# A fused vision block on one core: third image's turn, projection and skip products inside the scan, alternating PSUM tiles ahead of it

## The reference

```
x = x + L0(_gn(x))   # two depthwise 3x3 convs (g, g1), Sobel, 5 iterations of
                     #   h = D*(c0*h0 - 2*E*h + cm_x*roll(h,1,2) + cp_x*roll(h,-1,2)
                     #          + cm_y*roll(h,1,3) + cp_y*roll(h,-1,3)) + D*2*DT*fsrc, then bn + relu
x = x + L1(_gn(x))   # 3x3 conv, 64 -> 64 channels
x = x + L2(_gn(x))   # Mamba block: layernorm, in_proj (x and z), causal conv of 4 taps, silu,
                     #   dt/B/C projections, softplus, selective scan over 1024 tokens with 16 states,
                     #   y*silu(z), out_proj, + skip*x_norm, layernorm, proj
x = x + L3(_gn(x))   # 2-D DCT of 32 x 32
```

## Time and profile before

| | us |
|---|---|
| median of 3 runs (987.44 to 994.75) | 987.76 |
| the profiled execution | 989.86 |
| its span, first to last instruction | 987.7 |
| PE / DVE busy | 807.9 / 798.5 |
| ACT / POOL busy | 564.3 / 519.6 |
| mean granted TensorE clock, share of full speed | 0.948 |

### The profile page before, as it was taken

One profiled execution on the slowest core, in us unless ns is written; L12 is line 12 of the kernel. 1 busy time (PEld: TensorE's weight loads), 2 busy tenths in 40 slices (PEclk: granted clock), 3 DMA queues, 4 the chain that ended last, 5 costly groups with the idle time before them and its releaser, 6 DMA issues. The chain is left out here.

```text
span 987.7 us, 10385 instructions
## 1 busy us (share of the span) xinstructions
PE 807.9 (82%) x3787; PEld 509.9 (52%) x3787; DVE 798.5 (81%) x652; ACT 564.3 (57%) x983; POOL 519.6 (53%) x240
## 2 busy tenths in 40 slices
PE   3999998976576778799999999797756677869995
PEld 2444443443365667656545444344335577865654
DVE  6899885377998998998899888447699999899832
ACT  3755231146479897786667332114456979878712
POOL 2015993110498786876111699311048869677730
PEclk8999999999799999899999999898869989989988
DMA  3000000001535454443000000000123445444400
GB/s 104 1 0 0 0 0 1 0 1 48 133 134 180 153 181 163 140 159 130 20 0 11 12 0 0 1 0 1 48 89 127 175 148 184 160 148 154 146 21 22
DMA packets 32878, 73.95 MB, mean 75 GB/s; under 512 B 15544, under 2 KB 15680, under 8 KB 32832
## 3 DMA queue, kind: packets, MB, share of 16 engines
q1 hardware_dynamic: 31424, 72.04, 21.9%
q0 software_dynamic: 320, 1.05, 0.4%
q10 hardware_dynamic: 1088, 0.26, 0.1%
HBM read 70.71 MB, written 2.62 MB: 74 GB/s over the span
## 5 line engine op out<-in xcount | busy, mean ns | idle before, releaser
L338 POOL TENSOR_TENSOR arena<-arena 128x1024 f32<-128x1024 f32 x128 | 304.8, 2392 | 99.1 <-DVE arena L1603 72.8
L1603 DVE TENSOR_TENSOR_SCAN arena<-arena,ps 128x1024 f32<-128x1024 f32 x128 | 290.1, 2282 | 20.6 <-ACT arena L857 9.6
L857 ACT ACTIVATE arena<-arena 128x128 f32<-128x128 f32 (+3 forms) x424 | 157.1, 446 | 91.3 <-DVE arena L1530 75.3
L857 ACT ACTIVATE arena<-arena,Amat 128x1024 f32<-128x1024 f32 x128 | 145.3, 1145 | 62.0 <-DVE arena L1603 61.1
L544 PE MATMUL ps<-mat,arena 128*128 128x128 f32 x528 | 74.8, 288 | 51.6 <-DVE arena L1603 49.9
L857 ACT ACTIVATE arena<-ps 128x1024 f32<-128x1024 f32 (+2 forms) x62 | 56.1, 917 | 93.7 <-PE ps L414 29.0
L717 PE MATMUL ps<-arena,mat 128*128 128x512 f32 x240 | 106.3, 592 | 0.0
L586 PE MATMUL ps<-mat,arena 128*128 128x128 f32 x768 | 104.7, 281 | 1.1 <-POOL arena L338 0.8
L544 PEld LDWEIGHTS ps<-mat,arena 128*128 128x128 f32 x528 | 60.9, 144 | 67.3 <-DVE arena L1603 53.3
L586 PEld LDWEIGHTS ps<-mat,arena 128*128 128x128 f32 x768 | 90.9, 146 | 3.3 <-POOL arena L338 2.3
L1598 DVE TENSOR_TENSOR ps<-arena,ps 128x1024 f32<-128x1024 f32 x66 | 80.0, 1213 | 3.5 <-PE ps L544 3.5
(11 more groups left out here) (186 smaller groups left out, 1374.3 us busy)
## 6 DMA issues: line engine op xcount, KB each, us to landing
arena<-c_rows SPq DMA_DIRECT2D x128, 512.0 KB, 3.8
out<-arena SPq DMA_DIRECT2D x28, 64.0 KB, 2.2
xres<-x POOLq DMA_DIRECT2D x4, 256.0 KB, 5.3
xres<-x SPq DMA_DIRECT2D x4, 256.0 KB, 4.1
convw<-conv_w SPq DMA_DIRECT2D x1, 576.0 KB
c_rows<-ROWS SPq DMA_DIRECT2D x4, 128.0 KB, 1.9
mat<-mats SPq DMA_DIRECT2D x1, 448.0 KB, 3.7
inw<-in_w SPq DMA_DIRECT2D x1, 256.0 KB
```

The costliest lines, as they stand in the source:

```text
L338: tt(HC[s % 2], HS[s % 2], CB[s % 4], ALU.mult).then_inc(S("hc"), 1)
L857: return nc.scalar.activation(out_, in_, func, bias=bias, scale=scale, accum_out=accum_out)
L1603: nc.vector.tensor_tensor_scan(HS[q], DA[q], PS[q][:, :], 0.0, ALU.mult, ALU.add).then_inc(S("scan"), 1)
```

## The change

It edits these things at once:
- X_STEPS: for s from 9 to 25 the odd steps instead of s % 5 in (0, 2, 4), so 9 instead of 11 there.
- Ahead of the scan: new tiles `x_ps(k, b)` and `z_ps(k, b)` alternate with the image; `in_proj` is split into `x_in_proj` (second image waits for the first image's `silu_z`, semaphore sz) and `z_in_proj` (second image waits for rx); `bc_proj`, `keep_rows` and the first rows' turn use PS[2k] and PS[0]; the orders on TensorE, ScalarE and VectorE are rewritten; `relu_x(h, 1, 1)` moves behind `scan_step(h, 1)`; the spins go from 8 + 14 to 8 + 10 products.
- `bnout` of stage 0 writes PS[2k + 1] instead of the SBUF tile X, and `add_stage0` reads it there.
- Image 3 is turned too: `sum_of` takes the transposing form for all, `turn_y(h, 3)` and `keep_y(h, 3)` come before `out_proj(h, 3)`.
- Image 2 is turned at s = 49 (waits for X3) and kept by ScalarE at s = 51; the DCT of pair 0 moves up by one to three steps; `skip(1)` goes to s = 61 and `out_proj(h, 2)` to s = 62; TensorE waits for `y_kept(h, 2)` at s = 50.
- The centring's sums come at s = 38, `small_mean` at s = 40.
- Between the halves: `frames` before the first taps on ScalarE; `gate(3)` between Sobel's two parts; `write_all(PS[3])` and its wait (a_open 7) for `first_tap(1, 1, 0)`; `x_neighbours(h, 0)` directly behind `y_neighbours(h, 0)`; the second half's two rolls of pair 0 by 8 DMAs on SP's queue in place of two products and two copies; `from_D(h, 1)` stays behind `seed(h, 0)`.

```
-        X_STEPS = [s for s in range(9, SCANS - 1) if (s % 5 in (0, 2, 4) if s < 3 * D_STATE else s % 2 == 1)]
+        X_STEPS = [s for s in range(9, SCANS - 1) if (s % 5 in (0, 2, 4) if 26 <= s < 3 * D_STATE else s % 2 == 1)]
+        def x_ps(k, b):
+            return PS[2 * k + b]
+        def z_ps(k, b):
+            return PS[2 * k + 1 - b]
-        TURNED = [0, 1, 2]
+        TURNED = [0, 1, 2, 3]
...
+            def roll_by_dma(dst, src, up):
+                for g in (0, C):
+                    here, there = (g + 1, g) if up else (g, g + 1)
+                    sp.dma_start(dst[here:here + C - 1, :], src[there:there + C - 1, :]).then_inc(S("rolled"), 16)
+                    edge, other = (g, g + C - 1) if up else (g + C - 1, g)
+                    sp.dma_start(dst[edge:edge + 1, :], src[other:other + 1, :]).then_inc(S("rolled"), 16)
+            def roll_first_pair(h):
+                a = A[0]
+                sp.wait_ge(S("a_Py"), 4 * h + 2)
+                sp.wait_ge(S("a_Pm"), 2 * h + 1)
+                roll_by_dma(a["Kx"], a["Pmy"], up=False)
+                roll_by_dma(a["Ky"], a["R"], up=True)
@@ SyncE, end of a half @@
                 store_out(h, 0)
+                if h + 1 < HALVES:
+                    roll_first_pair(h + 1)
                 store_out(h, 1)
@@ TensorE, new calls @@
+            def x_in_proj(h, k, b):
+                pe.wait_ge(S("xnc"), 2 * h + k + 1)
+                if b == 1:
+                    pe.wait_ge(S(f"sz{k}"), 2 * h + b)
+                for n in range(2):
+                    last = mm(half(x_ps(k, b), n), inw[:, 2 * P * b:2 * P * b + P], half(D[k]["XNC"], n), start=True, stop=True)
+                last.then_inc(S(f"xi{k}"), 1)
+            def z_in_proj(h, k, b):
+                pe.wait_ge(S("xnc"), 2 * h + k + 1)
+                if b == 1:
+                    pe.wait_ge(S(f"rx{k}"), 2 * h + b)
...
@@ TensorE, ahead of the scan, the new order @@
+                group_mean(D[1], h, 2, 1)
+                spin(PS[1], 10)
+                n2_pixels(h, 1)
                 xn_channels(h, 0)
+                x_in_proj(h, 0, 0)
+                z_in_proj(h, 0, 0)
+                x_in_proj(h, 0, 1)
+                xn_channels(h, 1)
                 dt_proj(h, 0, 0)
+                x_in_proj(h, 1, 0)
+                z_in_proj(h, 1, 0)
                 dt_proj(h, 0, 1)
+                x_in_proj(h, 1, 1)
+                dt_proj(h, 1, 0)
+                z_in_proj(h, 0, 1)
+                z_in_proj(h, 1, 1)
                 bc_proj(h, 0)
                 turn_first_rows(h)
+                dt_proj(h, 1, 1)
                 pe.wait_ge(S("b_kept"), h + 1)
                 plain(pe)
                 b_rows(h, 0)
+                pe.wait_ge(S("rx0"), 2 * h + 2)
                 b_rows(h, 1)
                 bc_proj(h, 1)
                 b_rows(h, 2)
+                pe.wait_ge(S("rx1"), 2 * h + 2)
@@ TensorE, in the scan and behind it @@
+                    if s == 49:
+                        pe.wait_ge(S("X3"), 2 * h + 1)
                         turn_y(h, 2)
...
+                    if s == 50:
+                        y_kept(h, 2)
                         group_mean(D[0], h, 3, 0)
+                    if s == 52:
                         x3_pixels(h, 0)
+                    if s == 54:
                         first_dct(h, 0)
+                    if s == 56:
+                        a2_pixels(h, 0)
+                    if s == 57:
                         keep_x3(h, 0)
+                    if s == 58:
                         second_dct(h, 0)
+                    if s == 61:
+                        pe.wait_ge(S("ot"), 2 * h + 1)
+                        skip(1)
+                    if s == 62:
+                        out_proj(h, 2)
...
                 sum_of(h, SCANS - 1)
-                out_proj(h, 2)
+                turn_y(h, 3)
                 if h + 1 < HALVES:
                     depthwise(h + 1, 0, 0, 0)
                 out_proj(h, 3)
+                if h + 1 < HALVES:
+                    write_all(PS[3])
@@ VectorE, ahead of the scan, the new order @@
                 add_conv(h, 1)
+                x2_norm(h, 1)
                 normalize(0, h, 0)
                 center(1, h, 0)
                 variance(1, h, 0)
+                causal(h, 0, 0)
                 normalize(1, h, 0)
                 causal(h, 0, 1)
                 causal(h, 1, 0)
+                relu_x(h, 0, 0)
+                causal(h, 1, 1)
                 relu_x(h, 1, 0)
                 one_plus(h, 0)
                 one_plus(h, 1)
                 first_relu_part(h)
                 one_plus(h, 2)
+                relu_x(h, 0, 1)
                 delta(h, 0)
                 first_delta_u(h)
                 dve.wait_ge(S("first_du"), 2 * h + 2)
                 scan_step(h, 0)
                 delta(h, 1)
                 scan_step(h, 1)
+                relu_x(h, 1, 1)
                 delta(h, 2)
@@ ScalarE, ahead of the scan, the new order @@
                 norm2(h, 0)
                 square(h, 0, 0)
+                norm2(h, 1)
                 layer_scale(h, 0)
+                square(h, 1, 0)
                 silu_z(h, 0, 0)
                 silu_x(h, 0, 0)
                 layer_scale(h, 1)
                 silu_x(h, 0, 1)
                 silu_z(h, 1, 0)
+                abs_x(h, 0, 0)
                 abs_x(h, 0, 1)
                 silu_x(h, 1, 0)
                 abs_x(h, 1, 0)
+                silu_z(h, 0, 1)
                 for j in range(3):
                     exp_of(h, j)
                 silu_z(h, 1, 1)
                 silu_x(h, 1, 1)
+                keep_rows(h, 0)
+                ln_of(h, 0)
+                ln_of(h, 1)
+                keep_first_b(h)
+                ln_of(h, 2)
                 decay(h, 0)
                 keep_rows(h, 1)
                 decay(h, 1)
+                abs_x(h, 1, 1)
                 decay(h, 2)
@@ ScalarE, before the iteration loop, and stage 0's result @@
+                    if h > 0 and k == 0:
+                        act.wait_ge(S("rolled"), 128)
+                        act.sem_inc(S("a_Q5"), 1)
+                        act.sem_inc(S("a_Q6"), 1)
+                        act.wait_ge(S("a1_gg1"), 2 * h + 2)
+                        field(0)
+                        act.wait_ge(S("a_Pe"), 2 * h + 1)
+                        seed(h, 0)
+                        from_D(h, 1)
+                        continue
...
-                    av(img(a["X"]), wrapped(a["hw"])[:, :, 1:33], ACT.Relu, par[:, 4:5], par[:, 5:6]).then_inc(S("a_bnout"), 1)
+                    av(img(PS[2 * k + 1]), wrapped(a["hw"])[:, :, 1:33], ACT.Relu, par[:, 4:5], par[:, 5:6]).then_inc(S("a_bnout"), 1)
@@ ScalarE, end of a half @@
+                if h + 1 < HALVES:
                     act.wait_ge(S("X3"), 2 * h + 1)
                     zero_framed(h + 1, 0)
+                    frames(h + 1, 0)
                     first_tap(h + 1, 0, 0)
                     first_tap(h + 1, 0, 1)
+                    keep_y(h, 3)
                     squares(h + 1, 0)
                     zero_framed(h + 1, 1)
```

## The result

The changed kernel took **966.71 us** (median of 4 runs, 965.02 to 967.41) against 988.8 for the kernel before, measured beside it; the ratio is 0.976, 95% interval 0.973 to 0.980. Predicted were 966.0 and 957 to 979. The profiled execution took 966.85 us with a span of 964.9, so 22.8 us of span are to be explained. The total is right; most of its terms are not, and that their errors cancel to 1.1 us is luck.

A forecast was written before the change was run, and what follows sets the result against it. TensorE and VectorE were taken to share most of the span, GpSimd to bound the loop, with waits ahead of the scan. Terms 11.8 + 2.8 - 0.6 + 3.0 + 2.6 + 1.1 + 1.05 = 21.75 us gave 966.0, range 957 to 979.

The forecast's parts named there:

- Ahead of the scan: Conv's end to first scan: second image's product no longer waits for the first's `relu_x`; 5.9 us a half, 11.8 gained.
- The walk: New orders ahead of the scan timed instruction by instruction from the conv's end: first scan at 51.1 us, before 58.3.
- Stage 0's addition: VectorE's addition with one operand in PSUM takes 1.2 us; 1.9 gained in first half, 0.9 in second, 2.8 together.
- X steps: Scan: two fewer X steps a half add 4.9 us of multiplications, but waits for GpSimd go; net -0.6 us.
- Centring: In the scan, sums at s = 38 let scan 39 cover `small_mean`; 1.5 us a half, 3.0 gained.
- End of the scan: Image 3's sum takes 1.0 instead of 1.72 us, giving TensorE room for moved work; 2.6 us for both halves.
- Between the halves: Last scan of first half to second loop: loop starts 2.4 us earlier, 1.3 already counted, so 1.1 gained.
- The charge of 2 us for the clock: Between the halves: 2 us of TensorE work charged for running at 1.2 GHz after 5 us of idle.
- Tail: Last scan's end to the centring of pair 1: 8.75 us instead of 9.8, so 1.05 gained.
- Rival A: New order ahead of the scan waits elsewhere, half of 11.8 lost: 972, or 976 with X steps at worst; 22%.
- B: Between the halves, DMA rolls land late and hold up `field(0)` and the loop: 972, at the high bound 987; 9%.
- C: TensorE falls to 1.2 GHz ahead of the scan: +17 us a half, 1000, slower; 4%.

## Why the prediction was right, and where it wasn't

**Ahead of the scan, 11.8 forecast, 15.6 measured.** The mechanism is right: with its own tile the second image's product no longer waits. The step that fails is the choice of the value: the second half's 4.5 us stood in the bounds, not in the sum. The same instructions took 4.5 us longer there than in the first half before the change, at a clock of 0.86, where two of the second images' products took 3.75 and 3.28 us instead of 1.95. In the new order one group a half is slow (3.4 to 3.5 us), and VectorE loses 0.9 us to it or less. That the order does it is shown by the experiment on the order alone; why TensorE keeps the higher clock in it is not, for idle times of 2.49 and 2.86 us remain.

The walk itself was 2.0 to 2.4 us too short (51.1; 53.5 and 53.1 measured). In both halves 1.0 is missing at the start: VectorE waits 2.18 us for the turns of both pairs, which stand together ahead of the first x (12.4 instead of 11.4). In the second half a slow `dt(0,0)` holds the third `causal` back by 0.93. In the first half it was the place that the prediction named, `keep_rows(0)`: ScalarE waited 1.39 us there for slow products, and the first scan came 0.5 later than in the halves without it, not 2.

**Stage 0's addition, 2.8 forecast, 0.9 or less measured** by putting it back (0.5 and 0.4, inside what executions vary). The duration was right. The step "behind it stands `new_h(1)`, which waits for GpSimd's last addition: 1.9 remains" named the wrong releaser: TensorE's last product of the loop came later than GpSimd.

**X steps, -0.6 forecast, -2.3 in the two traces, -3.0 by putting them back (3.5 in the edited steps).** The traces' -2.3 holds a gain of 1.1 that is not theirs: in the second half the order ahead of the scan alone brings steps 2 to 26 from 77.21 to 76.07. The multiplications were counted right; the step that fails is the waits said to go with them. Those for GpSimd were to fall by 3.7 and fell by 0.9 in the first half and 0.6 in the second (2.2 to 1.6), and the wait of 1.39 for ScalarE at step 11, behind its two copies of the next half's input (290.53 to 292.76), is new.

**Centring, 3.0 forecast, 4.0 measured by putting it back.** 1.5 a half, as worked out, and some 0.4 more by step 50 that I had not counted.

**End of the scan, 2.6 forecast, 4.95 measured.** Half by the cheaper sums, half by the schedule. The sum took only the last wait of 1.23; four smaller ones in steps 57 to 61, 1.8 us a half together, gave place to one of 0.97.

**Between the halves, 1.1 forecast, 0.95 measured.** The loop starts 86.30 us behind the last scan instead of 87.25 (85.6 to 87.6 in the traces with this order, so the agreement proves little). The charge of 2 us for the clock, line 1526 at 1.22 us and the centring that stays all hold. GpSimd's two products, now beside operations of VectorE that read PSUM, took 2.20 us each instead of 3.05 and 3.19, and none of those operations was longer than 1.23, so the 2 us that the port rule might have cost did not arise. The rolls took 9.3 us, not 7.6 (5.5 us lie between SP's first and last issue), and filled the whole cover of 9.4. The sign "`field(0)` not released by a DMA" failed: ScalarE waited 1.81 us for the landing. The estimate of 18.4 us for the eight, one behind the other, came from the Trainium skill, "DMA: Bandwidth & Descriptors" ("Anatomy of one DMA"), whose figures are for transfers issued by GpSimd; these were issued by SyncE, and the traces show 9.3 and 10.5 us.

**Tail, 1.05 forecast, -1.26 measured.** The value that I set as a bound (-2, lower clock) was the case. The step that fails is the price of the three TensorE pieces: 1.0, 1.1 and 1.9 us in the sum, 1.94, 1.97 and 3.67 measured. The 5 us of idle that I priced between the halves stand here too, in pieces of 2.08, 1.32 and 1.11 us that I did not add up to anything.

So the sum is 1.1 us short of 22.8 because +3.8 (ahead), +1.2 (centring) and +2.4 (end of the scan) met -1.9 (first half's addition), -1.7 (X steps), -0.3 (second addition, between the halves) and -2.3 (tail). Rival A is out (9.3 us of waiting is left, not over 10), B came within 0.1 us of deciding, C is out: the clock ahead of the scan was 0.94 in both halves, and its slow products cost 0.5 to 0.9 us a half there. The range's low end is off as well: 966.0 less 4.5 and 3.2 is 958.3, not 957. And two halves of 1.25 at the end of the scan are 2.5, not 2.6.

## What to carry to other kernels

TensorE's clock is part of the schedule: moving real work out of a gap can cost as much as it saves. Unread products paid where every TensorE piece stands on the chain (the tail: 2.4 to 3.4 us for 13 of them, and 2.0 for ten more in the last stage); ahead of the scan they were worth 0.5 us a half at most, and between the halves nothing that the time shows. Ask of a filler which product it protects, and whether that product is the one that the slower branch waits for. When two halves of a kernel run the same instructions in different times, as here, the difference is a gain to be weighed in the forecast, and not only a bound. And a term is measured only if it is larger than what its stretch varies by without the edit.

## What was not expected of the hardware

- The granted clock of a stretch is a poor measure of its cost: 0.94 gave 53.05 to 53.56 us, 0.90 gave 53.34 and 53.54.
- Where TensorE idled 2.08, 1.32 and 1.11 us around short groups, they ran at 1.2 GHz; with idle times of 0.78, 0.45 and 0.46 between the same groups they ran at 2.4. The idle time alone does not tell: 13 unread products and 1.78 us of idle left the next group at 2.4 GHz (1.09 us) in one trace, and 1.80 us left it partly at 1.2 (1.56 us) in another.
- Eight DMAs within SBUF (four of 252 KB, four small) took SP 6.0 us to issue, 0.52 to 1.04 each, and landed 9.3 us behind the first issue; in another trace one issue took 1.95.
